# A transformer decoder layer: the self attention's q, k and v in three fp32r products, and the gate in four column tiles

## The reference, cut to what matters

```python
x = _layernorm(x + _L0_attn_ref(x, ...))
x = _layernorm(x + _L0_xattn_ref(x, ctx_1024, ctx_1024, ...))
x = _layernorm(x + _L0_ffn_ref(x, ...))
...
    qkv = (x @ W_qkv + b_qkv).reshape(B, S, 3, H, hd)
    q, k, v = (qkv[:, :, 0], qkv[:, :, 1], qkv[:, :, 2])
    attn = jnp.einsum('bqhd,bkhd->bhqk', q, k) / jnp.sqrt(jnp.asarray(hd, x.dtype))
    attn = jax.nn.softmax(attn, axis=-1)
    attn_out = jnp.einsum('bhqk,bkhd->bqhd', attn, v).reshape(B, S, D)
    gate = jax.nn.softmax(x @ W_gate + b_gate, axis=-1)
    top_g, top_i = jax.lax.top_k(gate, TOP_K)
    combine = jnp.sum(jax.nn.one_hot(top_i, E, dtype=x.dtype) * top_g[..., None], axis=2)
    expert_out = jnp.einsum('bsd,edf->bsef', x, W_experts) + b_experts
    moe_out = jnp.einsum('bsef,bse->bsf', expert_out, combine)
    return attn_out + moe_out
```

## Time and profile before

| | |
|---|---|
| median of 3 runs | 1357.91 us (1356.98 to 1358.36) |
| the profiled execution, its own time | 1358.7 us |
| span of its trace | 1356.9 us |
| TensorE matmul busy | 1251.6 us, 92% |
| VectorE busy | 903.9 us, 67% |
| ScalarE busy | 776.9 us, 57% |
| GpSimd busy | 364.8 us, 27% |
| granted TensorE clock, mean | 0.966 |

### The profile page before, as it was taken

How to read it: one execution, slowest core, us unless ns; L and a number is a source line. 1 busy time by engine, 2 the same in 40 slices (tenths; PEclk the granted TensorE clock), 3 DMA queues, 4 the chain that set the end, 5 groups by cost and what they waited for, 6 DMA issues and landing times.

```text
span 1356.9 us, 19260 instructions
## 1 busy us (share of the span) xinstructions
PE 1251.6 (92%) x6624; PEld 598.3 (44%) x6624; DVE 903.9 (67%) x1808; ACT 776.9 (57%) x1087; POOL 364.8 (27%) x435
## 2 busy tenths in 40 slices
PE   6789888999999999999999999999999999997995
PEld 3333344454444444444444544444444444443442
DVE  5367665566776767766777677767677677666672
ACT  2235554656657665656657565566556566564664
POOL 2300011321522225212243115222252123331162
PEclk9769988999999999999999999999999999998999
DMA  6804314134332144333223343431243333303300
GB/s 225 137 17 64 63 18 55 41 48 78 49 59 51 24 74 64 64 49 48 62 46 54 47 79 48 63 62 25 43 63 48 48 48 48 61 4 48 48 18 16
DMA packets 49840, 74.85 MB, mean 55 GB/s; under 512 B 8520, under 2 KB 20048, under 8 KB 49488
## 3 DMA queue, kind: packets, MB, share of 16 engines
q1 hardware_dynamic: 48736, 73.09, 33.1%
q10 hardware_dynamic: 1008, 0.53, 0.1%
HBM read 18.02 MB, written 4.19 MB: 16 GB/s over the span
## 4 chain that ended last, share of the span: by engine, by line
PE 77%; DVE 10%; issue 5%; ACT 4%; DMA 2%; SPq 1%; POOL 0%; DVEq 0%; ACTq 0%
PE ms L406 38%; PE sc L406 14%; PE op L406 14%; PE mx L406 7%; DVE maxes L808 4%; PE ms L425 2%; PE ms L480 2%; DVE k_parts L723 2%; ACT k_parts L600 1%; ACT probs L660 1%; DMA qs<-q_parts 1%; SPq L356 1%; DMA qs<-shift_r 1%; DVE x1b L764 1%; PE ms L475 1%
## 5 line engine op out<-in xcount | busy, mean ns | idle before, releaser
L808 DVE TENSOR_REDUCE maxes<-mx 128x1 f32<-128x512 f32 x1024 | 658.0, 684 | 362.4 <-PE mx L406 361.2
L660 ACT ACTIVATE probs<-sc 128x1024 f32<-128x1024 f32 x512 | 524.3, 1024 | 467.8 <-PE sc L406 463.3
L969 POOL TENSOR_TENSOR x<-x,moe 128x256 f32<-128x256 f32 x256 | 186.8, 730 | 643.6 <-ACT moe L653 618.6
L406 PE MATMUL op<-probs,v 128*32 128x512 f32 x2048 | 280.0, 619 | 2.2 <-ACT probs L660 1.1
L406 PE MATMUL sc<-qs,ks 50*128 50x512 f32 x1024 | 260.6, 506 | 11.1 <-ACT probs L660 7.7
L406 PEld LDWEIGHTS sc<-qs,ks 50*128 50x128 f32 x1024 | 96.9, 186 | 330.1 <-ACT probs L660 227.1
L406 PE MATMUL mx<-ks,qs 48*128 48x512 f32 x1024 | 211.9, 409 | 23.4 <-DVE maxes L808 15.3
L653 ACT ACTIVATE moe<-ms,comb 128x256 f32<-128x256 f32 x256 | 106.8, 472 | 17.6 <-PE ms L406 17.6
L406 PEld LDWEIGHTS mx<-ks,qs 48*128 48x128 f32 x1024 | 100.2, 192 | 31.5 <-DVE maxes L808 21.2
L406 PE MATMUL ms<-we_hi,x2T_hi 128*128 128x512 f32 x256 | 96.0, 456 | 6.3 <-DVE lin L742 3.5
L406 PEld LDWEIGHTS op<-probs,v 128*32 128x32 f32 x2048 | 40.9, 109 | 96.7 <-issue 94.8
(11 more groups left out here) (104 smaller groups left out, 1193.1 us busy)
## 6 DMA issues: line engine op xcount, KB each, us to landing
ks<-k_parts SPq DMA_DIRECT2D x192, 128.0 KB, 4.7
qs<-q_parts SPq DMA_DIRECT2D x192, 128.0 KB, 5.5
xT_s<-in_xT SPq DMA_DIRECT2D x8, 512.0 KB, 4.8
x_s<-in_x SPq DMA_DIRECT2D x8, 512.0 KB, 3.9
ctxT_s<-in_ctxT SPq DMA_DIRECT2D x8, 512.0 KB, 3.9
out<-x SPq DMA_DIRECT2D x7, 512.0 KB, 2.9
qs<-shift_r SPq DMA_DIRECT2D x128, 8.0 KB
probs<-in_we SPq DMA_DIRECT2D x1, 1024.0 KB, 7.7
```

The lines of the kernel that those rows point to most:

```text
L406: return nc.tensor.matmul(dst, lhsT, rhs, start=first, stop=last, skip_group_check=True)
L660: nc.scalar.activation(probs[:, (2 * s + h) % 3, :, :], sc[:], ACT.Exp).then_inc(exp_out, 1)
L808: nc.vector.tensor_reduce(maxes[:, g % 2, at:at + 1], mx[:, i % 3, :], AX_X, ALU.max).then_inc(max_out, 1)
L969: nc.gpsimd.tensor_tensor(x2[:, n % 2, t, :], x2[:, n % 2, t, :], moe[:, k % 2, j * D:j * D + D], ALU.add).then_inc(acc, 1)
```

## The change

- The x2T copy in plain float32 is gone. ScalarE writes `x2T_hi` alone; VectorE subtracts it from the bank into `x2T_lo`, which GpSimd did before. The bank is free only after VectorE.
- The weights `w_wqkv` become high and low parts `w3_hi` and `w3_lo`, made once at the start by ScalarE and GpSimd from two staging tiles.
- `k3c*` and `q3c*`: three fp32r products of two 512-column matmuls, six instructions instead of four. `v3a`, `v3b`: six fp32r matmuls of 256 columns for each block, twelve instructions instead of eight.
- `gate`: positions are now the moving side. The gate's weights, padded from 8 to 32 columns, are stationary in four column tiles, one for each block of 128 positions; high and low part of x2T are multiplied in plain float32. The result stands experts on partitions, so ScalarE copies it to `gateT` and a new unit `gateT` transposes it back.
- Tables: in `MID_LONG`, `gateT` comes at (30, 0), `g_exp` goes from (30, 0) to (31, 0) and `choose` from (30, 1) to (31, 0). In `MID_SHORT`, `gateT` comes at (24, 1).

```diff
-            "gate": (29, 0), "combT": (32, 0), ...
+            "gate": (29, 0), "gateT": (30, 0), "combT": (32, 0), ...
-            "apply23": (26, 0), "g_exp": (30, 0), "choose": (30, 1)}
+            "apply23": (26, 0), "g_exp": (31, 0), "choose": (31, 0)}
...
-        for c in range(DC):
-            halves["pool"][mid_at(f"x2T{c}", n) + 2].append((f"x2_low{c}", 1, n))
...
+            elif task in ("x2T0", "x2T1"):
+                eng.wait_ge(x2_low, DC * n + int(task[3]) + 1)
...
+            def project_parts(dst, wt, src, cols):
+                for m, (i, j) in enumerate(((0, 0), (1, 0), (0, 1))):
+                    for c in range(DC):
+                        last = mm(dst, wt[j][:, c, cols].bitcast(F32R), src[i][:, c, :].bitcast(F32R),
+                                  m == 0 and c == 0, m == 2 and c == DC - 1)
+                return last
+
+            def project_part_rows(bank, width, src, wt, cols, blocks):
+                for b, t in enumerate(blocks):
+                    for m, (i, j) in enumerate(((0, 0), (1, 0), (0, 1))):
+                        for c in range(DC):
+                            last = mm(bank[:, b * width:(b + 1) * width], src[i][:, c, t * P:(t + 1) * P].bitcast(F32R),
+                                      wt[j][:, c, cols].bitcast(F32R), m == 0 and c == 0, m == 2 and c == DC - 1)
+                return last
+
+            def gate_blocks(bank, src, wt):
+                for i in range(2):
+                    for c in range(DC):
+                        for t in range(TB):
+                            last = mm(bank[GATE_W * t:GATE_W * t + GATE_W, 0:P], wt[:, c, :], src[i][:, c, t * P:t * P + P],
+                                      i == 0 and c == 0, i == 1 and c == DC - 1)
+                return last
...
-                    last = project(bank, W["wqkv3"], x2T, slice(at, at + P))
+                    last = project_parts(bank, w3_part, x2T_part, slice(at, at + P))
...
-                    last = project_rows(bank, D, x2T, W["wqkv3"], slice(2 * D, 3 * D), (2 * h, 2 * h + 1))
+                    last = project_part_rows(bank, D, x2T_part, w3_part, slice(2 * D, 3 * D), (2 * h, 2 * h + 1))
...
-                    last = project_rows(bank, E, x2T, W["wg"], slice(0, E), range(TB))
+                    last = gate_blocks(bank, x2T_part, W["wg"])
+                elif task == "gateT":
+                    wait_unit_out(pe, "gate", n)
+                    last = nc.tensor.transpose(bank[:, 0:P], gateT, ident[:])
...
-                    c = int(task[3])
                     wait_unit(act, task, n)
-                    copy(x2T[:, c, :], bank)
-                    copy(x2T_part[0][:, c, :].bitcast(F32R), bank).then_inc(done, 1)
+                    copy(x2T_part[0][:, int(task[3]), :].bitcast(F32R), bank).then_inc(x2_high, 1)
+                elif task == "gate":
+                    wait_unit(act, task, n)
+                    copy(gateT, bank[:, 0:P]).then_inc(done, 1)
...
+                elif task in ("x2T0", "x2T1"):
+                    c = int(task[3])
+                    dve.wait_ge(x2_high, DC * n + c + 1)
+                    nc.vector.tensor_tensor(x2T_part[1][:, c, :].bitcast(F32R), bank, x2T_part[0][:, c, :],
+                                            ALU.subtract).then_inc(x2_low, 1)
```

More of the change, by code:

```diff
@@ L83 @@
 UNITS_LIN = ("q1", "k1", "v1", "s0", "s1", "s23", "o1", "y01", "y23", "x0", "x1", "kc0", "qc0", "cv0", "cv1", "kc1", "qc1")
-UNITS_MID = ("hT0", "hT1", "cy0", "cy1", "x2T0", "x2T1", "k3c0", "q3c0", "gate", "k3c1", "q3c1", "v3a", "v3b",
+UNITS_MID = ("hT0", "hT1", "cy0", "cy1", "x2T0", "x2T1", "k3c0", "q3c0", "gate", "gateT", "k3c1", "q3c1", "v3a", "v3b",
              "combT", "be0", "be1")
@@ L146, in own_signal @@
 def own_signal(task):
-    return task in SPLITS or task in ("be0", "be1", "shift", "heads", "gate") or task.startswith("moe")
+    return task in SPLITS or task in ("be0", "be1", "shift", "heads", "gateT", "x2T0", "x2T1") or task.startswith("moe")
 TAKEN = {unit: sum(not own_signal(ORDER[v][0]) for v in range(u % 2, u + 1, 2)) for u, unit in enumerate(ORDER)}
@@ L214, in sem @@
             return ctx.enter_context(nc.semaphore(name))
-        W = {name: sb("w_" + name, list(ap.shape)) for name, ap in w.items() if name != "we"}
+        W = {name: sb("w_" + name, list(ap.shape)) for name, ap in w.items() if name not in STAGED}
         ident = W["ident"]
@@ L231, in decoder @@
         combT = o1T[0:E, :]
+        gateT = sb("gateT", [P, P])[:]
         x1 = sb("x1", [P, TB, D])
@@ L265, in decoder @@
         we_part = (sb("we_hi", [P, DC, E * D]), sb("we_lo", [P, DC, E * D]))
+        w3_part = (sb("w3_hi", [P, DC, 3 * D]), sb("w3_lo", [P, DC, 3 * D]))
+        w3_stage = (heads[:].rearrange("p n d -> p (n d)").rearrange("p (c d) -> p c d", c=DC),
+                    moe[:, 0, :].rearrange("p (c d) -> p c d", c=DC))
+        W3_COLS = (slice(0, 2 * D), slice(2 * D, 3 * D))
         we_stage = (probs[:].rearrange("p s h t -> p (s h t)")[:, 0:E * D],
@@ L294, in decoder @@
         G_STEPS = 12
-        LATE = tuple(n for n in w if n not in FIRST + EARLY and n != "we")
+        LATE = tuple(n for n in w if n not in FIRST + EARLY + STAGED)
         block = ctx.enter_context(nc.Block())
@@ L388, in _ @@
                 sp.dma_start(W[name][:], w[name]).then_inc(w_late, 16)
+            for k in range(2):
+                sp.dma_start(w3_stage[k], w["wqkv3"][:, :, W3_COLS[k]]).then_inc(w3_in, 16)
             for c in range(DC):
@@ L702, in _ @@
                         copy(we_part[0][:, c, :].bitcast(F32R), we_stage[c]).then_inc(we_cut, 1)
+                    for k in range(2):
+                        copy(w3_part[0][:, :, W3_COLS[k]].bitcast(F32R), w3_stage[k]).then_inc(w3_cut, 1)
                 if t == 0:
                     act.wait_ge(we_cut, 2 * DC)
+                    act.wait_ge(w3_cut, 4)
                 if 0 <= s < SLOTS * len(PHASES):
@@ L789, in take_out @@
                                             ALU.mult).then_inc(heads_out, 1)
[L790 removed]
+                elif task in ("x2T0", "x2T1"):
[3 more added lines that the diff above has]
+                                            ALU.subtract).then_inc(x2_low, 1)
+                elif task == "gateT":
                     wide = [P, TB, E]
                     wait_unit(dve, task, n)
[L793 removed]
+                    nc.vector.tensor_tensor(g_p[:], bank[:, 0:P].rearrange("p (n e) -> p n e", n=TB)[:, :, 0:E],
                                             W["bg"][:].rearrange("p (o e) -> p o e", o=1).broadcast_to(wide),
@@ L984, in _ @@
                                                 ALU.subtract).then_inc(we_cut, 1)
+                    pool.wait_ge(w3_cut, 2)
+                    for k in range(2):
+                        nc.gpsimd.tensor_tensor(w3_part[1][:, :, W3_COLS[k]].bitcast(F32R), w3_stage[k],
+                                                w3_part[0][:, :, W3_COLS[k]], ALU.subtract).then_inc(w3_cut, 1)
                 for task, k, n in OTHERS["pool"][t]:
@@ L1027 @@
         "bv3": rows(bqkv[2 * D:]),
-        "wg": by_chunk(arr(ffn + "W_gate")), "bg": rows(arr(ffn + "b_gate")),
+        "wg": np.pad(by_chunk(arr(ffn + "W_gate")), ((0, 0), (0, 0), (0, P // TB - E))), "bg": rows(arr(ffn + "b_gate")),
         "we": by_chunk(arr(ffn + "W_experts").transpose(1, 0, 2).reshape(D, E * D)),
```

23 lines of the change are left out of this document (13 added, 10 removed), and 4 rows, old and new, of tables (MID_LONG, MID_SHORT).

## The result

The change makes the kernel slower: median 1372.54 us (1360.76 to 1373.98, 11 executions) against 1358.36 (1356.98 to 1363.64, 11) run beside it, ratio 1.0071, 95% interval 1.004 to 1.0102. I had said 1359.2, range 1351 to 1367: the median lies outside. The executions of the change fall in two groups here: four at 1360.8 to 1361.9, with a mean granted clock of 0.962 to 0.965, and seven at 1372.0 to 1374.0, with 0.953 to 0.955. Of the runs further down, one execution of parts_only (1786.88 us, mean clock 0.596) and one of the kernel before (1441.23, 0.825) were slow as a whole and are left out of the ratios. The profiled one is of the first group: 1361.22 us, span 1359.4, where I had 1360.0 for it.

A forecast was written before the change was run, and what follows sets the result against it. TensorE, busy 92% of the span, was taken to bound the kernel. Savings of 6.8, 3.5 and 4.8 against 13.6 of waits gave -1.5 us; clock terms -2.8 and +5.6 made it +1.3, so 1359.2 us, range 1351 to 1367.

The forecast's parts named there:

- The units: On TensorE, cheaper k and q units save 6.8 us, v units 3.5 and the gate 4.8.
- The new gate: Column tiles run side by side: 1.0 us instead of 1.81, saving 0.8 in each of sequences 1 to 6.
- The waits: TensorE waits for VectorE behind `gateT` and for the later choose, costing 13.6 us together.
- `gateT`'s place: In sequences 1 to 5, `v1` waits for VectorE's copy of `shift`, lengthening the half-slot by 1.53 us.
- choose's place: Choose follows the next reduces; `mx` of (32, 0) waits 2.2 us; with `gateT`'s place 2.57 more, five times.
- Sequence 6: No `v1` there; choose starts a half-slot later, costing 0.7 us.
- the clock: Half-clock falls behind four of six new `mx` waits cost 5.6 us, at 1.4 each.
- The rival that the clock falls at every new wait: Six 2.2 us waits and some behind `gateT`, nine falls at 1.4 us: 1366.2, slower; chance 0.21.
- The clock's gain at the gate: With the dense gate, both half-clock falls behind the old gate (sequences 1 and 6) go: -2.8 us.
- The rule weighed: Tiling changes drain TensorE: 16 more at 0.17 us would add 2.7, giving 1361.9; the prediction went by the rows instead.
- Sequences 0 and 7: Gate and c0 units save nothing there, ahead of a DMA wait; four c1 units save 0.31 us each.

The follow-up runs named there:

- parts_only: The change's fp32r q, k, v units and VectorE low part, but the old gate, on `x2T_hi` alone, without `gateT`: 1354.96 us, 0.9952 of the kernel before.
- split kernels: Kernels with choose cut in two, its last five operations at (31, 1), built on the kernel before, the change or parts of it: medians 1337.10 to 1358.02 us.
- both_early: The change with `gateT` moved to (29, 1) behind k1 and `g_exp` and choose to (30, 1): 1349.42 us, 0.9896 of the kernel before.
- before_choose_late: The kernel before with choose alone moved from (30, 1) to (31, 0): 1367.71 us, 1.0051 of the kernel before.
- after: The change itself in its first set of runs: median 1372.54 us, 1.0071 of the kernel before; the profiled execution took 1361.22 us.
- after_again: The change without an edit, run and profiled again: 1368.46 us, 1.0043 of the kernel before; the profiled execution took 1360.50 us.
- after_look: The change without an edit, profiled once more: this execution took 1368.52 us at a mean clock of 0.959.
- gateT_early: The change with `gateT` alone moved from (30, 0) to (29, 1) behind k1, choose left late: 1358.53 us, 0.9979 of the kernel before.
- choose_early: The change with `g_exp` and choose moved from (31, 0) to (30, 1), `gateT` left in place: 1348.11 us, 0.9895 of the kernel before.
- split_gateT_late: The change with `g_exp` and choose at (30, 1), choose's last five operations at (31, 1), `gateT` at (30, 0): 1346.46 us, 0.9893 of the kernel before.
- before_split: The kernel before with choose cut in two, its last five operations at (31, 1): 1358.02 us, 0.9982 of the kernel before.
- parts_split: parts_only with choose cut in two: 1346.27 us, 0.9887 of the kernel before.

## Why the prediction was wrong

**The units were right.** q 1.59 alone (1.60 forecast), v 1.62 (1.69; spacing 0.118 instead of 0.124). The new gate takes 795.43 - 794.42 = 1.01 (1.0 forecast). At full clock the fp32r parts are worth 156.90 - 155.54 = 1.36 a sequence, and 1.41 and 1.46 from the split kernels; the gate with its `gateT` unit 156.10 - 155.46 = 0.64 to 154.69 - 154.00 = 0.69, where I had 0.8 without counting the 0.12 that `gateT` itself takes. That 1.36 was hit to the hundredth is luck in part. Alone, a v unit saves 1.92 - 1.62 = 0.30, where I had 0.22 (and 1.92 - 1.69 is 0.23); but v3a stands at (38, 1) between `shift` and `heads`, as k3c0 and k3c1 do, and its half-slot goes from 3.05 (before) to 2.89 (parts_only), 0.16 less. v3b's goes from 3.62 to 3.30. I had not seen that the place halves the gain of every second v unit.

**The waits were right.** `gateT`'s place 1.53 (1.53 forecast), choose's place 1.11 (1.04). With 1.41 and 0.69 saved, 156.90 - 1.41 - 0.69 + 1.53 + 1.11 = 157.44; the change shows 157.47. My sum, 156.90 - 1.36 - 0.80 + 1.53 + 1.04, gives 157.31. Both places together are worth 157.47 - 154.93 = 2.54 (2.57 forecast). What each is worth depends on the other, though: from the change, undoing choose's place alone wins 1.80 (157.47 - 155.67), and `gateT`'s after it only 0.74 (155.67 - 154.93), since the pair of waits of 0.64 and 0.69 then comes back. Sequence 6 was near by luck. From its (30, 1) to its (32, 1) the change takes 10.58, against 9.61 in both_early, whose order is there that of the kernel before: 0.97 more, where I had 0.7 for choose. But choose late makes it shorter (9.30 in before_choose_late), and what makes it longer is a wait that I had left out, 1.24 us of `heads` behind `gateT`.

**The step that failed is the clock**: "I take more than half, four of six: +5.6", at 1.4 us each. The number of falls was near enough: in the four profiles with choose late and the new units (after, after_again, after_look, gateT_early) a fall follows 15 of the 24 `mx` waits. What was mis-sized is the price. Where the clock goes down while `mx` still waits (0.08 to 0.35 us before it starts, four times in after_look, twice in gateT_early), the fall lasts 6.8 us and costs 2.9; where it goes down 0.3 to 1.8 us behind the start, it lasts 3.4 and costs 1.5; and at nine waits there is none. I had given every fall the length of those behind the gate. The trace of before had a longer one to read: the earlier trace rows show only the first 3.4 us of the low clock at the wait of 184.82. It goes on to 193.9, 10.2 us in all (the granted clock is third from the end):

```profile
187.10:190.50 3.40, 3.01 (x15) 1.65 (x12) 1.48 (x3) 2.87 (x6) 0.00 (x0) 0.50 0.00 0
190.50:193.90 3.40, 3.40 (x16) 1.90 (x18) 0.54 (x1) 1.40 (x3) 1.27 (x1) 0.50 0.02 5
```

Falls also need not come one by one with a chance each: in after_look, gateT_early and parts_only they come four or five sequences in a row, in after and after_again they do not. So I had priced an average, with the spread of a few independent falls, where the times on record reach from 1360.5 to 1374.0. The rival that the clock falls at every new wait comes nearest in time, but it counted nine falls at 1.4 (1366.2), and `v1`'s wait behind `gateT` is followed by none in 25 sequences (the wait of `heads` in sequence 6 by one in choose_early and one in split_gateT_late).

**What the median adds** can be counted, as an estimate, from the mean clock on record for every execution. It is 0.9635 over the four short ones and 0.9539 over the seven long ones, which in their spans is 99 and 127 us at half clock. A fall of 6.8 us costs 2.9, so 27 us more cost some 12 us, and the groups lie 11.8 apart. Nothing else is needed to tell them apart. A profile that has this much is not on record, but two together do: after_look has 112 us at half clock and a short end, 242.7 us behind sequence 6's (30, 1), 23 of them at half clock; with the end of the first profile, 247.0 and 38, it would have 127 and take 1372.8.

**The clock's gain at the gate was right in kind.** In nine profiles with the new gate, none of 54 gates of sequences 1 to 6 is followed by a fall; in five with the old one, nine of 30 are (with sequences 0 and 7, none of 72 against 16 of 40). The earlier trace rows had shown two.

**The rule weighed.** At the 0.17 us a change that I had tried for it, the two changes of tiling around the gate would have put it at 1.34 instead of 1.0; it is at 1.01. The Trainium skill (TensorEngine Tiling (Array Packing), Key Properties) says that changing the tiling mode drains TensorE. A drain of that size does not show here, and I was right to go by the rows; a smaller one is not excluded, since four rounds of streaming are 0.85 of the 1.01.

**Sequences 0 and 7** moved by the clock as well. Up to sequence 1's (30, 1), before had 68 us at half clock and took 331.2 us; the change 58 and 325.1. Of these 6 us, some 3 are the clock's: before_split, with the old units and 58 us, took 327.9. The end is slower instead: 38 us at half clock behind sequence 6's (30, 1) against 21, 247.0 us against 242.9. I had not priced that; in after_look the same end takes 242.7.

**Open**: what decides which kind an execution is. No profile is of an execution of the group at 1372 (the lowest clock in a profile of the change is 0.959, theirs is 0.953 to 0.955). That they have more half clock is on record, and that it accounts for their time is counted above; that it lies in the same places, longer falls in sequences 1 to 5 and a slow end, is argued from after_look and the first profile, and not shown. Open too is what makes the clock fall at a wait: the `mx` wait of the late choose is followed by a fall in one of six sequences of before_choose_late and in 15 of 24 with the new units.

## What to carry to other kernels

Price a wait on TensorE twice: once by its length and once by the fall of the clock that it can bring, which here cost 1.5 or 2.9 us at a wait of 2.1, and ask what the time is if every repetition of the loop has it, since in some executions the falls came in step with the loop. Take the length of a fall from one at a wait of that kind, and follow it to its end. Read the mean clock beside each time before comparing two kernels, and compare stretches at full clock to see what an edit is worth. When a change moves a long job on a second engine, look for the places where that engine is idle and cut the job to fit: here that, with `gateT` moved, took 35 us off the first median of the change and 31 off the second. In the kernel before, the same cut alone won nothing that can be told.

## What the runs showed of the hardware

- The granted clock fell behind TensorE's waits of 0.6 and 0.7 us in a row (parts_only, both_early; not in before), not only behind those of 2 us, and behind a unit of sixteen instructions with 8 columns each in which TensorE showed as busy throughout (parts_split).
- The length of a wait did not tell what the clock does. At the 1.8 us `mx` wait of sequence 0 there was a fall of 10.2 or 13.7 us in all fourteen profiles; near the 84 waits of 1.3 us for `heads` in them (six in each) there was none.
- At the same 2.1 us `mx` wait there was no fall, one of 3.4 us or one of 6.8 us, and the long ones had begun inside the wait (behind `heads`, in choose_early, one of 6.8 us began after it); with a fall in each, sequences last 160.4 (after_look) or 157.0 us (parts_only) and the next fall lies in almost the same place.
- Sixteen column-tiled float32 matmuls of 128 columns by 32 (32 instructions) took 1.01 us, 0.03 an instruction (after); fp32r matmuls were spaced 0.118 us at 256 columns and 0.23 at 512 (after).
